# A deformable convolution behind a pair block: all sampling pairs of a unit ahead of the convolution of the same unit

## The chip, the cores and the metric

One core of one Trainium2 chip runs the whole program. The metric is device time in microseconds (us); a lower number is better. TensorE (PE) multiplies matrices, VectorE (DVE), ScalarE (ACT) and GpSimd (POOL) work elementwise, SyncE (SP) issues DMAs. Each engine runs its own list of instructions strictly in order, and waits at semaphores for the others.

## The reference

The input x has the shape (2, 128, 128, 128): 2 images, 128 channels, 128 x 128 pixels. Two layers are computed, each behind a group norm (32 groups of 4 channels) and each added to its input:

```
x = x + pair_block(group_norm(x))     # a, b, sigmoid gate: three 128x128 products,
                                      # a @ b per channel row, gate, product with Wo
x = x + deform_conv(group_norm(x))
def deform_conv(x):
    x = relu(x)
    offset = conv3x3(x, w_off) + b_off          # 18 channels: (y, x) for each of 9 taps
    py, px = pixel + tap + offset               # sampling places
    samp   = bilinear(x, py, px)                # zero outside the image
    return sum over channels and taps of samp * w_def
```

## The kernel before, in words

The first stage (about a fifth of the time) does the pair block in 64 groups and writes the sum to `x1_pad`. The second stage, the bands, does the deformable convolution and is what the change touches. An image is cut into 16 bands of 8 rows and each band into 2 sides of 64 columns: 64 units of 512 pixels for both images.

For one unit n, the steps are named by letters in a written list, `ORDER` (L404). All engines walk the same list; `bands` (L426) calls, for each step, only the function that the engine has for its letter. `ahead` (L428) says for which unit a letter works in turn n of the outer loop, relative to n. The letters:

- `h` near pixels: ScalarE norms and rectifies the 10 x 66 pixels around the unit (`cast_z`, L950), casts them to `z_hi` (L938), and VectorE makes the remainder `z_lo` (L1310).
- `O` offsets: TensorE convolves `z_hi` and `z_lo` with `woff` (L805), ScalarE takes the result out (L961).
- `P` VectorE splits the offsets into two float16 parts (L1273, L1276). `Q` TensorE turns them into distances between every sampling place and every pixel of its window (`locate`, L742 and L744), ScalarE takes their absolute value (`dist`, L970).
- `G` VectorE makes the bilinear hat functions (`hats`, L1284). `H` ScalarE's queue issues two DMAs that write them to memory (`store_hats`, L976). `R` VectorE takes the farthest distance (L1289), which the kernel looks at after the last band: no unit is far here, and a general path behind it doesn't run.
- SyncE spreads the hats over partitions (`spread_hats`, L545: three groups of three taps), GpSimd multiplies the y and x hats into `weights`, nine products a unit (`k`, `weigh`, L1541). Their first product waits until all pairs of the unit two before are sampled.
- `z` ScalarE makes `z`, the 22 overlapping windows of a unit (`make_z`, L927). `T` TensorE turns them, four windows a group and two in the last (L777); the groups are copied to `zT` by ScalarE (T0, T2, T4, L994) and VectorE (T1, T3, T5, L1319). A group's bank is free when the copy of the group two before is done.
- `s` sampling, eleven pairs of windows: four matmuls (L759) write a bank. ScalarE copies the high float16 part (`copy_samples`, L985), VectorE the low part (`copy_samples_lo`, L1300). Three banks take turns, so pair p waits for the low part of pair p - 3 (`lows_ready`, L755).
- `c` the nine taps of the convolution, three matmuls each (`conv`, L731). The first waits for all low parts of its unit. After the last, VectorE adds the input rows and writes `y` (`add_x1`, L1334).

Samples, weights and windows have two buffers each (`u = n % 2`), `zT`, the near pixels and the hats one. Rows of the input stand in a ring of 11 blocks of 4 rows (`raw`); SyncE loads a block when the unit that read its predecessor last has its `y` (L524), and stores a finished band (L533). Before the change the convolution works one unit behind the sampling (`"c": -1`), with taps written between the pairs. No planner is at work; the order is the one written out.

Of the kernel before, what the change touches and what calls it, by code (L numbers as in the profile page):

```python
# [7 lines left out]
P = 128  # L8
# [11 lines left out]
RPI, SIDES = HH // BR, WW // UW  # L20
BPI = RPI * SIDES
BANDS = IMGS * BPI
# [11 lines left out]
AHEAD = 3  # L34
# [64 lines left out]
def preact_conv_kernel(nc, x, Wa, ba, Wb, bb, Wg, bg, Wo, bo, w_off, b_off, w_def,  # L99
                       ident_d, group_mask_d, select_d, select_all_d, coords_d, out):  # L100
    with ExitStack() as ctx:
        def sb(name, shape, dt=F32):
            return ctx.enter_context(nc.sbuf_tensor(name, shape, dt))
# [63 lines left out]
        z = sb("z", [P, 2, WINDOWS, SRC_R, SRC_C])  # L167
# [15 lines left out]
        s6 = sb("s6", [P, BATCH, 6])  # L183
# [212 lines left out]
        def sampled_pair(b):  # L396
# [5 lines left out]


        ORDER = [(step[0], int(step[1:])) for step in (  # L404
            "h0 s0 s1 s2 k0 h1 c0 c1 T0 k1 s3 s4 z0 z1 O0 k2 s5 c2 c3 T1 k3 s6 P0 s7 c4 T2 k4 c5 s8 Q0 "
            "c6 k5 G0 T3 s9 k6 H0 c7 T4 k7 s10 c8 T5 k8 R0").split()]

        def hats_landed(n):

# [7 lines left out]
        def last_unit(block):  # L417

            b = min(block % BLOCKS // (BR // RB), RPI - 1)
            return block // BLOCKS * BPI + b * SIDES + SIDES - 1  # L420
# [4 lines left out]

        def bands(eng, stages):  # L426

            ahead = {"c": -1, "s": 0, "k": 1, "T": 1, "z": 2, "h": 3, "O": 3, "P": 3, "Q": 3,  # L428
                     "G": 3, "H": 3, "R": 3}
            for n in range(-AHEAD, BANDS + 1):  # L430
                for kind, j in ORDER:
                    m = n + ahead[kind]
                    if kind in stages and 0 <= m < BANDS:
                        stages[kind](m, m % 2, j)

        block = ctx.enter_context(nc.Block())
# [3 lines left out]
        def _(sp):  # L440
# [78 lines left out]
            def load_block(block):  # L519

                if block >= IMGS * BLOCKS:
                    return
                if block >= RING:
                    sp.wait_ge(y_ready, last_unit(block - RING) + 1)  # L524
                slot = block % RING
                sp.dma_start(raw[:, slot * RB:(slot + 1) * RB, :].rearrange("p r w -> p (r w)"),
                             x1_pad[block // BLOCKS, :, block % BLOCKS * RB:(block % BLOCKS + 1) * RB, :]
                             .rearrange("c r w -> c (r w)")).then_inc(raw_in[slot], 16)

            def store_y(n):  # L530
                b = n // SIDES
                sp.wait_ge(y_ready, n + 1)
                sp.dma_start(out_v[b // RPI, :, b % RPI * BR * WW:(b % RPI + 1) * BR * WW],  # L533
                             y[:, b % 2, :]).then_inc(y_out[b % 2], 16)

            def spread_hats(n):


                sp.wait_ge(*hats_landed(n))
                for g in range(TROWS):  # L540
                    wait(sp, weights_ready, TAPS * (n - 1) + TROWS * (g + 1))
                    rows = [hat_rows[0][n % AHEAD, g, g:g + NEAR_R].rearrange("(r o) c -> r o c", o=1),
                            hat_rows[1][n % AHEAD, g].rearrange("(o r) c -> o r c", o=1)]
                    for dst, src in zip((hy_flat, hx_flat), rows):
                        sp.dma_start(dst[g * SRC_C:(g + NEAR_R) * SRC_C,  # L545
                                         g * CHUNK:(g + 1) * CHUNK],
                                     src.broadcast_to([NEAR_R, SRC_C, CHUNK])
                                     ).then_inc(hat_in[g], 16)
# [4 lines left out]
            spread_hats(0)  # L553
            spread_hats(1)

            for n in range(BANDS + 2):
                if n >= 2 and n % SIDES == 1:
                    store_y(n - 2)
                for block in range(IMGS * BLOCKS):
                    if last_unit(block) == n - 2:  # L560
                        load_block(block + RING)
                if n + 2 < BANDS:
                    spread_hats(n + 2)
# [35 lines left out]
        def _(pe):  # L599
# [137 lines left out]
            def locate(n, u, _):  # L737

                pe.wait_ge(off_split, n + 1)
                wait(pe, dist_ready, n)  # L740
                for axis in range(2):
                    nc.tensor.matmul(pairs[0][:, axis, :], select[:, axis, :],  # L742
                                     offs_hi[:], start=True, stop=False)
                    mm = nc.tensor.matmul(pairs[0][:, axis, :], select[0:CONST_AT, axis, :],  # L744
                                          offs_lo[0:CONST_AT, :], start=False, stop=True)
                mm.then_inc(located, 1)
# [64 lines left out]
            def offsets(n, u, _):  # L811
                pe.wait_ge(z_hi_ready, n + 1)
                wait(pe, dist_ready, n)
                convolve_offset_parts(n).then_inc(off_done, 1)

            pe.wait_ge(select_set, SELECT_STEPS)
            pe.wait_ge(scaling, W_STEPS)
            bands(pe, {"c": conv, "Q": locate, "s": sample, "T": turn_windows, "O": offsets})


# [47 lines left out]
        def _(act):  # L868
# [89 lines left out]
            def evict_offsets(n, u, _):  # L958
                act.wait_ge(off_done, n + 1)
                wait(act, off_split, n)  # L960
                nc.scalar.activation(offs4[0:CONST_AT, :], bank[B_OFF][0:CONST_AT, :], ACT.Identity,  # L961
                                     bias=bias_off[0:CONST_AT, :],
                                     scale=unscale[0:CONST_AT, OFF:OFF + 1]
                                     ).then_inc(off_evicted, 1)
# [23 lines left out]
            def copy_windows(n, u, g):  # L988
                if g % 2:
# [8 lines left out]
            act.wait_ge(scaling, W_STEPS)  # L998
            act.wait_ge(final, FINAL_STEPS)
            bands(act, {"Q": distances, "H": store_hats, "s": copy_samples, "T": copy_windows,  # L1000
                        "z": make_z, "h": cast_z, "O": evict_offsets})


        @block.vector
        def _(dve):
# [316 lines left out]
            def add_x1(n, u, k):  # L1322
# [7 lines left out]
                for r0, r1, src in ((0, whole, at), (whole, BR, 0)):  # L1330
                    if r0 == r1:
# [10 lines left out]

            dve.wait_ge(scaling, W_STEPS)
            bands(dve, {"c": add_x1, "P": split_offsets, "G": make_hats, "R": reach_of,
                        "s": copy_samples_lo, "T": copy_windows, "h": split_z})

# [248 lines left out]
```

## Time and profile before

| | |
|---|---|
| median of 3 runs | 1642.09 us (1631.22 to 1646.17) |
| profiled execution | 1645.54 us, span 1643.7 us |
| TensorE, matmuls | busy 1543.9 us, 94% of the span |
| VectorE | 1111.5 us, 68% |
| ScalarE | 1052.1 us, 64% |
| GpSimd | 934.0 us, 57% |
| granted TensorE clock | 0.986 of full speed in the mean |
| band stage | first sampling matmul at 384.15 us, last tap at 1636.74 us |

Busy time is a union of an engine's instructions over the span. Matmuls are pipelined: one of 512 columns lasts 0.38 us from start to end, but the next starts 0.22 us after it. So on TensorE the differences of starts count, not durations. A row's idle time is time in which its engine did nothing ahead of it, and the arrow names what ended the wait.

### The profile page before, as it was taken

What the parts mean: (1) busy time and instruction counts of PE and PEld (TensorE: products, weight loads), DVE (VectorE), ACT (ScalarE), POOL (GpSimd) and SP (SyncE); (2) the same over time, 40 slices, a digit from 0 to 9 for tenths busy, and PEclk for the clock granted to TensorE, in tenths of its full rate; (3) what the DMA queues carried; (4) which work ended last, traced back from release to release, by engine and by line L of the source; (5) the groups of instructions that cost most, each with busy time, mean ns of one, the idle gap of its engine ahead of it and who ended that gap; (6) DMA issues with size and microseconds to landing.
All of it is one profiled execution on the core that took longest, in us unless ns stands there. A gap on an engine that the chain in (4) does not pass through costs nothing.

```text
span 1643.7 us, 28193 instructions
## 1 busy us (share of the span) xinstructions
PE 1543.9 (94%) x9875; PEld 1129.6 (69%) x9876; DVE 1111.5 (68%) x1910; ACT 1052.1 (64%) x1500; POOL 934.0 (57%) x734
## 2 busy tenths in 40 slices
PE   4999999937999999999999999999999999999997
PEld 3777787715776667776666676766777677767775
DVE  5988888745666666666666666666666666666653
ACT  2555555527676767767667666666777777666662
POOL 2555555716755555655665656566566566656562
PEclk9999999958999999999999999999999999999999
DMA  4343344246767777777776777777767777777672
GB/s 138 107 119 106 118 118 118 75 166 241 262 260 247 253 240 268 252 253 246 247 251 243 242 252 255 246 249 272 261 237 256 254 256 268 261 243 247 242 238 67
DMA packets 145701, 356.56 MB, mean 217 GB/s; under 512 B 10709, under 2 KB 77808, under 8 KB 145584
## 3 DMA queue, kind: packets, MB, share of 16 engines
q1 hardware_dynamic: 130864, 327.90, 59.1%
q10 hardware_dynamic: 14720, 27.14, 4.7%
q8 instruction: 69, 1.13, 0.3%
q14 instruction: 48, 0.39, 0.1%
HBM read 292.14 MB, written 62.85 MB: 216 GB/s over the span
## 4 chain that ended last, share of the span: by engine, by line
PE 61%; issue 12%; POOL 8%; DVE 8%; DMA 6%; ACT 2%; SPq 0%; ACTq 0%; POOLq 0%; DVEq 0%
PE bank L759 24%; PE pair L731 17%; PE pair L805 7%; DMA hx_all<-hat_x 6%; POOL samples_hi L1496 4%; PE bank L777 4%; DVE offs_lo L1276 3%; PE pair L777 3%; POOL weights L1541 2%; DVE offs_hi L1273 2%; PE pair L742 2%; PE pair L744 2%; ACT samples_hi L985 1%; POOL rstd L1470 1%; POOL samples_lo L1483 1%
## 5 line engine op out<-in xcount | busy, mean ns | idle before, releaser
L1541 POOL TENSOR_TENSOR weights<-hy_all,hx_all 126x512 f32<-126x512 f32 x576 | 756.6, 1343 | 522.0 <-DMA hx_all<-hat_x 381.6
L1300 DVE SCALAR_TENSOR_TENSOR samples_lo<-bank,samples_hi 128x432 f16<-128x432 f32 (+1 forms) x704 | 403.4, 591 | 364.7 <-ACT samples_hi L985 351.5
L759 PE MATMUL bank<-weights,zT 126*128 126x216 f32 (+1 forms) x2816 | 583.0, 344 | 2.7 <-POOL weights L1541 2.3
L759 PEld LDWEIGHTS bank<-weights,zT 126*128 126x128 f32 x2816 | 490.2, 190 | 44.0 <-issue 29.2
L985 ACT ACTIVATE samples_hi<-bank 128x432 f16<-128x432 f32 (+1 forms) x704 | 362.4, 519 | 226.3 <-PE bank L759 216.2
L731 PE MATMUL pair<-samples_hi,w_hi 128*128 128x512 f16 x576 | 218.9, 380 | 1.2 <-DVE y L1334 1.2
L731 PE MATMUL pair<-samples_lo,w_hi 128*128 128x512 f16 x576 | 217.7, 378 | 0.0
L731 PE MATMUL pair<-samples_hi,w_lo 128*128 128x512 f16 x576 | 217.6, 378 | 0.0
L994 ACT COPY zT<-pair 126x512 f32<-126x512 f32 x192 | 112.5, 586 | 112.2 <-PE pair L777 108.0
L927 ACT ACTIVATE z<-raw,norm_band 128x2772 f32<-128x2772 f32 (+3 forms) x80 | 180.0, 2270 | 0.0
L1483 POOL TENSOR_TENSOR samples_lo<-samples_hi,samples_lo 128x512 f16<-128x512 f32 x64 | 74.2, 1159 | 131.1 <-ACT samples_lo L888 131.0
L879 ACT ACTIVATE samples_hi<-pair,nbias,rstd 128x512 f32<-128x512 f32 x64 | 49.8, 778 | 135.3 <-PE pair L630 84.3
L777 PEld LDWEIGHTS pair<-ident,z 128*126 128x126 f32 x768 | 96.2, 141 | 36.9 <-issue 0.5
L1319 DVE COPY zT<-bank 126x512 f32<-126x512 f32 (+1 forms) x192 | 113.9, 593 | 5.0 <-PE bank L777 5.0
L777 PE MATMUL pair<-ident,z 128*126 128x128 f32 x768 | 116.1, 274 | 0.0
L950 ACT ACTIVATE abg_space<-raw,norm_band 128x660 f32<-128x660 f32 (+2 forms) x74 | 104.9, 1431 | 16.9 <-DMA raw<-x_pad 12.4
L777 PEld LDWEIGHTS bank<-ident,z 128*126 128x126 f32 x640 | 81.7, 140 | 40.3 <-DVE zT L1319 2.7
L805 PE MATMUL pair<-z_hi,woff 128*64 128x512 f16 x576 | 87.5, 412 | 17.8 <-ACT z_hi L938 17.8
L777 PE MATMUL bank<-ident,z 128*126 128x128 f32 x640 | 101.8, 274 | 2.3 <-DVE zT L1319 2.3
L731 PEld LDWEIGHTS pair<-samples_lo,w_hi 128*128 128x128 f16 x576 | 55.5, 96 | 69.0
L970 ACT ACTIVATE dist<-pair 128x1024 f32<-128x1024 f32 x64 | 65.6, 1025 | 57.0 <-PE pair L744 57.0
L1284 DVE TENSOR_SCALAR hats<-dist 128x1024 f32<-128x1024 f32 x64 | 52.4, 819 | 68.1 <-ACT dist L970 68.1
(138 smaller groups left out, 1944.8 us busy)
## 6 DMA issues: line engine op xcount, KB each, us to landing
hy_all<-hat_y SPq DMA_DIRECT2D x192, 648.0 KB
hx_all<-hat_x SPq DMA_DIRECT2D x192, 648.0 KB
raw<-x_pad SPq DMA_DIRECT2D x68, 272.0 KB, 11.2
x_pad<-hy_all SPq DMA_DIRECT2D x64, 272.0 KB, 3.3
weights<-in_x SPq DMA_DIRECT2D x64, 256.0 KB, 2.9
out<-y SPq DMA_DIRECT2D x32, 512.0 KB, 10.6
hat_y<-hats ACTq DMA_DIRECT2D x64, 252.0 KB
hat_x<-hats ACTq DMA_DIRECT2D x64, 162.0 KB
```

The source lines that it names most:

```text
L731: mm = nc.tensor.matmul(bank[B_CONV], w_part[:, k, :], part[:, u, k, :], start=(k == 0 and (w_part, part) == (w_hi, samples_hi)), stop=(k ...
L759: mm = nc.tensor.matmul(sampled_pair(b)[:, :, at:at + BR * cols], zT[0:WPIX, w, :], weights[0:WPIX, u, :, w * WC * BR:(w * WC + cols) * BR ...
L777: mm = nc.tensor.transpose(bank[B_ZT[g % 2]][0:WPIX, (w % 4) * P:(w % 4 + 1) * P], z[:, u, w].rearrange("p r c -> p (r c)"), ident[:])
L805: mm = nc.tensor.matmul(bank[B_OFF][at:at + width, :].rearrange("p (w r) -> p w r", r=BR), woff[:, k, 0:width], pixels[:, kx:kx + UW, ky:k ...
L927: done = nc.scalar.activation(z[:, u, :, rows, :], patches, ACT.Relu, bias=norm_band[:, 1].rearrange("p b n -> p (b n)")[:, n:n + 1], scal ...
L950: done = nc.scalar.activation(z_near[:, :, r0:r1], raw[:, src:src + r1 - r0, left:left + UW + 2].rearrange("p r w -> p w r"), ACT.Relu, bi ...
L985: nc.scalar.activation(samples_hi[:, u, :, c0:c1], sampled_pair(b)[:, :, 0:c1 - c0], ACT.Copy).then_inc(samples_ready, 1)
L994: nc.scalar.copy(zT[0:WPIX, 4 * g:4 * g + c, :].rearrange("p w c -> p (w c)"), bank[B_ZT[0]][0:WPIX, 0:c * P]).then_inc(zT_a, 1)
L1300: nc.vector.scalar_tensor_tensor(out=samples_lo[:, u, :, c0:c1], in0=sampled_pair(b)[:, :, 0:c1 - c0], scalar=1.0, in1=samples_hi[:, u, :, ...
L1319: nc.vector.tensor_copy(zT[0:WPIX, 4 * g:4 * g + c, :].rearrange("p w c -> p (w c)"), bank[B_ZT[1]][0:WPIX, 0:c * P]).then_inc(zT_v, 1)
L1483: nc.gpsimd.tensor_tensor(xT_lo[:], xT[:], xT_hi[:], ALU.subtract).then_inc(xT_lo_ready, 1)
L1541: nc.gpsimd.tensor_tensor(weights[0:WPIX, u, k, :], hy_all[0:WPIX, k, :], hx_all[0:WPIX, k, :], ALU.mult).then_inc(weights_ready, 1)
```

## The change

The list `ORDER` is written anew: the eleven pairs of a unit come first, then the offsets, then the nine taps of the same unit (`"c": 0`), among which turns, offsets, locating and distances lie. The near pixels are made four units ahead in place of three, at the end of the turn in place of its start and middle. The outer loop begins one turn earlier and ends one earlier. SyncE's stores and row loads follow the convolution, which is one turn earlier by the loop's count.

```diff
         ORDER = [(step[0], int(step[1:])) for step in (
-            "h0 s0 s1 s2 k0 h1 c0 c1 T0 k1 s3 s4 z0 z1 O0 k2 s5 c2 c3 T1 k3 s6 P0 s7 c4 T2 k4 c5 s8 Q0 "
-            "c6 k5 G0 T3 s9 k6 H0 c7 T4 k7 s10 c8 T5 k8 R0").split()]
+            "s0 s1 k0 s2 s3 k1 s4 s5 k2 s6 s7 k3 s8 s9 s10 O0 k4 z0 z1 c0 c1 T0 P0 c2 T1 k5 c3 c4 T2 Q0 c5 T3 "
+            "G0 k6 c6 h0 T4 H0 c7 k7 h1 T5 c8 k8 R0").split()]
...
-            ahead = {"c": -1, "s": 0, "k": 1, "T": 1, "z": 2, "h": 3, "O": 3, "P": 3, "Q": 3,
+            ahead = {"c": 0, "s": 0, "k": 1, "T": 1, "z": 2, "h": 4, "O": 3, "P": 3, "Q": 3,
                      "G": 3, "H": 3, "R": 3}
-            for n in range(-AHEAD, BANDS + 1):
+            for n in range(-AHEAD - 1, BANDS):
                 for kind, j in ORDER:
...
-            for n in range(BANDS + 2):
-                if n >= 2 and n % SIDES == 1:
-                    store_y(n - 2)
+            for n in range(BANDS + 1):
+                if n >= 2 and n % SIDES == 0:
+                    store_y(n - 1)
                 for block in range(IMGS * BLOCKS):
-                    if last_unit(block) == n - 2:
+                    if last_unit(block) == n - 1:
                         load_block(block + RING)
```

## Rows read from the trace of the kernel before

**Rows 1.** Busy time by stretch, band stage: PE, PEld, DVE, ACT, POOL, clock, DMA share, GB/s

```profile
1160.00:1360.00 200.00, 199.24 (x1188) 142.52 (x1184) 131.72 (x208) 141.47 (x200) 119.29 (x92) 1.00 0.74 251
```

**Rows 2.** Timeline of TensorE, one turn: start us, duration us, engine, line, operation

```profile
1197.06 1.32 PE L805 MATMUL pair<-z_hi,woff 128*64 128x512 f16 x9
...
1199.12 1.00 PE L759 MATMUL bank<-weights,zT 126*128 126x216 f32 x4
...
1205.61 0.38 PE L742 MATMUL pair<-offs_hi,select 117*128 117x512 f16 x1
...
1206.49 0.38 PE L731 MATMUL pair<-samples_hi,w_hi 128*128 128x512 f16 x1
...
1209.39 0.70 PE L759 MATMUL bank<-weights,zT 126*128 126x216 f32 x4
1209.93 0.38 PE L731 MATMUL pair<-samples_hi,w_hi 128*128 128x512 f16 x1
...
1210.58 0.38 PE L777 MATMUL bank<-ident,z 128*126 128x128 f32 x2
1210.80 2.36 PE L759 MATMUL bank<-weights,zT 126*128 126x216 f32 x12
1212.99 0.38 PE L731 MATMUL pair<-samples_hi,w_hi 128*128 128x512 f16 x1
...
1216.28 1.32 PE L805 MATMUL pair<-z_hi,woff 128*64 128x512 f16 x9
```

**Rows 3.** Timeline of ScalarE, the same turn; idle time before in brackets

```profile
1197.59 2.74 ACT L927 ACTIVATE z<-raw,norm_band 128x2772 f32<-128x2772 f32 x1
1200.23 0.78 ACT L961 ACTIVATE offs<-pair,bias_off,unscale 114x512 f32<-114x512 f32 x1
...
1206.69 1.02 ACT L970 ACTIVATE dist<-pair 128x1024 f32<-128x1024 f32 x1 [0.34 <-PE pair L744]
1208.51 0.53 ACT L985 ACTIVATE samples_hi<-bank 128x432 f16<-128x432 f32 x1 [0.79 <-PE bank L759]
...
1209.59 0.59 ACT L994 COPY zT<-pair 126x512 f32<-126x512 f32 x1 [0.56 <-PE pair L777]
...
1210.44 1.59 ACT L950 ACTIVATE abg_space<-raw,norm_band 128x660 f32<-128x660 f32 x1
...
1213.62 0.75 ACT L938 ACTIVATE z_hi<-abg_space 128x660 f16<-128x660 f32 x1
```

**Rows 4.** Timeline of ScalarE and its DMA queue, in the ramp of the bands

```profile
383.26 0.31 ACTq L976 DMA_DIRECT2D hat_y<-hats  x1
383.61 0.45 ACTq L976 DMA_DIRECT2D hat_x<-hats  x1
384.10 0.59 ACT L994 COPY zT<-pair 126x512 f32<-126x512 f32 x1 [1.60 <-DVE hats L1284]
```

**Rows 5.** Timeline of VectorE, an undivided y; T5's copy and R lie between

```profile
1191.73 0.74 DVE L1334 SCALAR_TENSOR_TENSOR y<-pair,unscale,raw 128x512 f32<-128x512 f32 x1
...
1193.55 1.64 DVE L1300 SCALAR_TENSOR_TENSOR samples_lo<-bank,samples_hi 128x432 f16<-128x432 f32 x3
```

**Rows 6.** By line, 420 to 1600 us: ns min/median/max; and a timeline row of GpSimd

```profile
L1284 DVE TENSOR_SCALAR hats<-dist x59: 693/695/1677, 438.0 to 1578.5; 128x1024 f32<-128x1024 f32 x59
L1276 DVE TENSOR_TENSOR offs_lo<-offs,offs_hi x59: 691/1634/1645, 434.1 to 1574.9; 114x512 f16<-114x512 f32 x59
L1310 DVE TENSOR_TENSOR z_lo<-abg_space,z_hi x59: 835/1098/1946, 425.0 to 1566.0; 128x660 f16<-128x660 f32 x59
...
1152.10 11.74 POOL L1541 TENSOR_TENSOR weights<-hy_all,hx_all 126x512 f32<-126x512 f32 x9 [3.57 <-PE bank L759]
```

**Rows 7.** Timeline of TensorE: a locate in the ramp, the first pairs, the last tap

```profile
380.39 0.39 PE L742 MATMUL pair<-offs_hi,select 117*128 117x512 f16 x1 [2.06 <-DVE offs_lo L1276]
...
384.15 2.36 PE L759 MATMUL bank<-weights,zT 126*128 126x216 f32 x12
...
1636.74 0.38 PE L731 MATMUL pair<-samples_lo,w_hi 128*128 128x512 f16 x1
```

## The prediction

> **What bounds the kernel now.** First the stretches of busy time: in 200 us of the band stage TensorE is busy 199.24 us at a granted clock of 1.00, VectorE 131.72, ScalarE 141.47, GpSimd 119.29 [rows 1]. So TensorE's own list of work sets the length of a turn there, and the other engines have 60 to 80 us of slack in 200. Whether that slack lies in the right place is what the change alters. Second, TensorE's timeline of one turn: it issues without a hole for 19.22 us [rows 2]. From the differences of starts: offsets (O) 2.06 us; locate (Q) 0.88; one tap of the convolution, three matmuls, 0.65; a group of two window turns 0.22, so 0.43 for four; three sampling pairs 2.19, so 0.73 a pair; the short last pair 0.54. A turn is then 2.06 + 9 x 0.65 + 5.5 x 0.43 + 0.88 + 10 x 0.73 + 0.54 = 19.0 us, and no order of it can be shorter. Third, ScalarE and VectorE in the same kind of turn [rows 3 to 5]: what each pair needs behind TensorE, and what else these two do between pairs.
>
> **What the change does to a turn.** No instruction is added or removed. All eleven pairs s0 to s10 come first, then O, nine taps among T0 to T5, Q, and the rest. Pair p writes one of three banks and waits until VectorE has taken the low part of pair p-3 (`lows_ready`). Before, taps lie between pairs and give ScalarE and VectorE time; after, three pairs may run and the fourth has to wait for the chain of the first.
>
> *The sampling run by itself.* From the start of a pair: 0.73 + 0.17 until its result is out (the row of twelve matmuls ends 0.17 after the next start [rows 2]), 0.53 high part on ScalarE [rows 3], 0.61 low part on VectorE (the last of the three in 1.64 us, which follow each other by 0.52 [rows 5]), with 0.03 to 0.05 at each hand-over: 2.15 us, against 2.19 for three pairs. So the run costs nothing as long as both engines are free for it. The join s10 to c0 costs nothing either: high and low of the short pair take about 1.2 us, and O covers them with 2.06 (in the last turns, which have no O, that cover is gone and c0 comes 1.25 us late).
>
> *The rest of the turn, which now stands in one block.* I walk it from the start of O, t = 0. **TensorE** if nothing is late: O to 2.06, c0 c1 to 3.36, T0 3.79, c2 T1 4.87, c3 c4 6.17. **ScalarE**: the offsets leave at 2.06 + 0.17 + 0.03 = 2.26, for 0.77 [rows 3]; z0/z1 2.74 us, started 0.1 before its predecessor ends as there, so 2.93 to 5.67; only then the copy of T0, 5.57 to 6.16. T2 waits for it: 6.21 to 6.64 on TensorE, 0.04 late. Q to 7.52. (VectorE's P0 is done in time: from 3.06 a cast and offs_lo, each at most the 1.64 us of [rows 6], give 6.4, and Q starts at 6.64.) Distances 1.02 from 7.72 to 8.74; h0 1.59, 8.64 to 10.23; T4's copy 0.59, 10.13 to 10.72 (turned at 9.88); H0, the two DMA issues of the hats, which stand in ScalarE's queue: from the first issue to the next instruction 0.84 [rows 4], so 10.75 to 11.59; h1's z_hi 0.75 [rows 3], to 12.34. **VectorE** is behind that in order: h1's z_lo, then T5's copy, y (needs c8), the reach R0, and only then the low part of s0 of the next unit. z_lo from 12.37; I take 1.25 us, between the median 1.10 and the longest 1.95 [rows 6], since GpSimd will run there more often (below): 13.62. y, T5's copy and R0 together take 1.82 us up to the next low part from the start of y to that of the low parts [rows 5]; another order, the same sum: 13.54 to 15.36. Low part of s0: 15.97. s3 can start at 16.0.
>
> TensorE without this wait: c5 T3 c6 T4 to 9.68, c7 T5 c8 to 11.20, s0 s1 s2 to 13.39. So **s3 stands for 2.6 us in every turn**, with the whole of TensorE's queue behind it. Low parts of s1 and s2 follow at 0.52 us, faster than the pairs, and the rest of the run is undisturbed: s3 to s10 take 7 x 0.73 + 0.54 = 5.65. The new turn is 16.0 + 5.65 = **21.65 us** against 19.0 of pure work. Pieces of z, near pixels and y split at the end of the ring of rows add something; 0.1 a turn is my estimate, 21.75.
>
> *Moves past queues.* GpSimd may start the products of the unit after next when all eleven pairs of a unit are sampled (`sampled`); that point comes nearly at the start of the block, where it was late in the turn. Nine products take 11.74 us [rows 6], and are now due a whole turn later: no cost by itself. SyncE's store and row loads are renumbered by one with the convolution; they wait for the same y at the end of a turn, next to the hats that SyncE needs anyway: nothing. The earlier near pixels ask for ring rows whose predecessors were freed three turns or more before: nothing.
>
> *Locks between VectorE and GpSimd.* The rows show hats at 0.69 us in the median and 1.68 at most, offs_lo 0.69 to 1.64, z_lo 0.84 to 1.95 [rows 6]. An undisturbed product of GpSimd is 1.30 us (11.74 / 9), and every excess is at most about that. As the nine products now begin near t = 0.2, they cover the block up to t = 12 or later, where offs, hats and z_lo lie. Hats run from 9.35 (after T3's copy): at 0.7 us they end before H0 could be issued, at 1.68 they end at 11.03 and push H0 by 0.3. Without any such delay z_lo takes 0.84 and the turn is 21.2; with the full one at both places it is 21.65 + 0.3 + 0.7 = 22.65.
> The Trainium skill ("SBUF — State Buffer", the section on the shared port pair) says that VectorE and GpSimd hold one pair of ports as an exclusive lock for a whole instruction and the loser blocks fully. The spread of those rows agrees. It speaks against this change, as it makes the long end (22.65) the more likely one; the sum above stays at the value between.
>
> **The sum.** The first pair starts at 384.15 and the last tap's last matmul at 1636.74 [rows 7]; 1643.7 - 1636.96 = 6.74 us follow. Nothing ahead of the first pair changes materially. After: 384.15 + 7.84 (first eleven pairs) + 60 turns with near pixels and offsets x 21.75 = 1305 + one turn without near pixels 19.2 + two without offsets and locate 17.35 each (1.25 + 5.85 + 2.4 + 7.84) + the last nine taps 1.25 + 5.85 + 6.74 = 1764.7. The profiled execution took 1645.5 for a span of 1643.7, so 1.8 more: about **1767 us**; its own time is 0.2% above the median of the three runs, which I ignore. Ends: turn 20.5, if no lock bites (21.2) and the 0.84 of the DMA issues holds nothing up: 1692 us. Turn 22.8 with full locks and split pieces: 1830.
>
> **Rivals.**
> (a) *The block fits, and TensorE stays full.* Mechanism: if ScalarE and VectorE get through the block 2.6 us sooner, s3 never waits, and the small holes before Q vanish as well. The turn is 19.03: 1767 - 60 x 2.72 = 1604 us. It decides at one point: the low part of s0 must be done by 13.35, where I have 15.97. For it: 60 us of slack in 200. Against: the chain O, z, T0, T2, Q, distances, near pixels, H0, z_hi, z_lo, tail is serial, each link measured. 0.06.
> (b) *Half of it fits.* The wait is 0.3 to 0.8 us a turn, and the gain of fewer holes before Q eats it: 1625 to 1655. 0.05.
> (c) *The clock falls.* TensorE now pauses once a turn. In the ramp it had idled 2.06 us before a locate which ran at 0.39 us a matmul, the full clock [rows 7]; I expect 2.6 to behave alike. If the sampling behind the wait ran at half clock, it took 5.65 us more a turn: 1767 + 339 = 2106. 0.03.
> [...]
> (d) *The wait comes, of another size.* Short (1692 to 1735, no locks, issues cheap) 0.17; as summed (1735 to 1800) 0.52; long (1800 to 1830) 0.17.
>
> **Numbers.** About 1% is what a measurement of this kernel can tell from no change. (d) and (c) are slower: 0.89. (b) is mostly within 1%: 0.05. (a) is faster: 0.06. The range 1692 to 1830 holds (d), 0.86, and leaves out the rest.
>
> **What would show it.** Right: in every turn the fourth pair (L759) idles 2 to 3.5 us, released by VectorE's low part; just ahead of it VectorE runs z_lo, zT, y, farthest, low part without a hole; TensorE is at about 88% in the stage; no hole before Q; granted clock still 1.00; GpSimd released by TensorE in nearly all turns. Wrong: low part of s0 directly behind its high part, or holes elsewhere (T2 or T4 waiting for zT, sampling waiting for weights). The prediction fails if ScalarE does not hold up z_hi until the hats are issued, or if z_lo and the tail of VectorE overlap more than their rows say.

## The result and the profile after

The changed kernel takes 1846.01 us in the median of 6 runs (1834.02 to 1852.09); the kernel before, now also with 6 runs, 1640.76 us. The ratio is 1.1229, with a 95% interval of 1.1186 to 1.1272. Medians are over all runs and ratios over the fast ones alone, since a program now and then runs about a per cent slower, whatever the kernel. The forecast was slower, 1767 us, range 1692 to 1830: the direction and the wait of the fourth pair came true, the clock did not, and the size lies outside the range. The profiled execution took 1852.1 us, 85.6 more than the sum of 1766.5 that the prediction made for it.

First the page of the changed kernel (span, TensorE's busy time, and the sampling matmuls with the idle time ahead of them), and the stretch of 200 us that answers to [rows 1]:

```profile
span 1850.3 us, 28193 instructions
...
PE 1630.8 (88%) x9875; PEld 1202.5 (65%) x9876; DVE 1133.6 (61%) x1910; ACT 1068.4 (58%) x1500; POOL 953.3 (52%) x734
...
L759 PE MATMUL bank<-weights,zT 126*128 126x216 f32 (+1 forms) x2816 | 611.5, 378 | 144.8 <-DVE samples_lo L1300 136.7
```

```profile
1200.00:1400.00 200.00, 181.92 (x1031) 130.32 (x1030) 117.03 (x177) 125.11 (x173) 113.93 (x84) 0.97 0.64 221
```

TensorE idles 136.7 us for VectorE's low parts, where it had 0.4 before. Its share is 88% of the span and 90% over the 60 turns with offsets, near the 88% expected. But that is 137 us, and the span is 207 us longer; and the granted clock, 1.00 before, is 0.97 in this stretch and 0.95 over the 60 turns. The timeline of TensorE shows both losses. Two turns, each from its fourth pair (the row with the idle time in brackets) over the offsets (L805) to the three pairs ahead of the next wait:

```profile
1199.48 6.18 PE L759 MATMUL bank<-weights,zT 126*128 126x216 f32 x32 [1.39 <-DVE samples_lo L1300]
1205.60 1.32 PE L805 MATMUL pair<-z_hi,woff 128*64 128x512 f16 x9
...
1216.77 2.35 PE L759 MATMUL bank<-weights,zT 126*128 126x216 f32 x12
1221.12 7.73 PE L759 MATMUL bank<-weights,zT 126*128 126x216 f32 x32 [2.00 <-DVE samples_lo L1300]
1228.79 1.32 PE L805 MATMUL pair<-z_hi,woff 128*64 128x512 f16 x9
```

The same eight pairs take 6.12 us up to the next offsets behind a pause of 1.39 us, and 7.67 behind one of 2.00. In three short stretches around the second (columns as in [rows 1]):

```profile
1219.12:1221.12 2.00, 0.01 (x1) 0.00 (x0) 1.94 (x4) 0.53 (x1) 2.00 (x3) 1.00 0.28 113
...
1221.12:1224.20 3.08, 3.08 (x12) 2.94 (x13) 1.91 (x4) 1.06 (x2) 1.19 (x1) 0.69 0.95 311
1224.20:1228.79 4.59, 4.59 (x23) 4.16 (x22) 2.72 (x5) 2.62 (x5) 0.00 (x0) 0.84 0.74 259
```

The clock is granted in full during the pause; behind it, the mean is 0.69 and then 0.84 of full speed, a mix of the two levels of 2.4 and 1.2 GHz. I took the 58 turns from 443.99 to 1781.46 us apart in this way; a turn here runs from one start of the offsets to the next. Mean turn 23.06 us: fourth pair at 15.88 us after the start of the offsets, pause 2.28 (1.39 to 3.33), and from the fourth pair to the next offsets 7.18. The last number is 6.11 in 21 turns and 7.5 to 9.0 in 37; the latter are called slow below.

Why the fourth pair waits: ScalarE and VectorE in the turn from 1205.60 (t = 0).

```profile
1211.08 0.57 ACT L994 COPY zT<-pair 126x512 f32<-126x512 f32 x1
1212.41 0.59 ACT L994 COPY zT<-pair 126x512 f32<-126x512 f32 x1 [0.76 <-PE pair L777]
1213.29 1.02 ACT L970 ACTIVATE dist<-pair 128x1024 f32<-128x1024 f32 x1 [0.29 <-PE pair L744]
1214.21 1.62 ACT L950 ACTIVATE abg_space<-raw,norm_band 128x660 f32<-128x660 f32 x1
1215.70 0.31 ACTq L976 DMA_DIRECT2D hat_y<-hats  x1
1215.72 0.59 ACT L994 COPY zT<-pair 126x512 f32<-126x512 f32 x1
1216.05 0.34 ACTq L976 DMA_DIRECT2D hat_x<-hats  x1
1216.49 0.75 ACT L938 ACTIVATE z_hi<-abg_space 128x660 f16<-128x660 f32 x1 [0.18 <-issue]
```

```profile
1217.28 1.45 DVE L1310 TENSOR_TENSOR z_lo<-abg_space,z_hi 128x660 f16<-128x660 f32 x1 [1.61 <-ACT z_hi L938]
1218.65 0.41 DVE L1319 COPY zT<-bank 126x256 f32<-126x256 f32 x1
1218.99 0.73 DVE L1334 SCALAR_TENSOR_TENSOR y<-pair,unscale,raw 128x512 f32<-128x512 f32 x1
1219.75 0.68 DVE L1289 TENSOR_REDUCE farthest<-dist 18x1 f32<-18x512 f32 x1
1220.46 1.64 DVE L1300 SCALAR_TENSOR_TENSOR samples_lo<-bank,samples_hi 128x432 f16<-128x432 f32 x3
```

This is the chain that the prediction walked, link by link. ScalarE has only 0.18 us of holes between distances and z_hi, and VectorE none from z_lo to the first low part, which ends at 1221.1 and releases the fourth pair at 1221.12. (A lock is what the prediction calls it when VectorE's and GpSimd's instructions lengthen each other.) One turn later it shows: hats take 1.52 us, the DMA issues start 0.58 after the start of T4's copy (0.02 before it in the turn above), z_hi waits 0.81 "for hats", and the pause becomes 2.83. Of these 0.83 us more, 0.2 are the near pixels (L950), which run in two pieces here. In 10 of 59 turns z_hi waits for the hats, 10.5 us in all.

```profile
1238.18 1.52 DVE L1284 TENSOR_SCALAR hats<-dist 128x1024 f32<-128x1024 f32 x1
1239.15 0.57 ACT L994 COPY zT<-pair 126x512 f32<-126x512 f32 x1
1239.73 0.31 ACTq L976 DMA_DIRECT2D hat_y<-hats  x1
...
1240.52 0.75 ACT L938 ACTIVATE z_hi<-abg_space 128x660 f16<-128x660 f32 x1 [0.81 <-DVE hats L1284]
```

### The profile page after: what moved, and what is told of

The parts are those of the page before. It is cut to its first block, busy times and chain, and to the rows that moved or that the text cites. A ratio compares the mean times of both kernels' runs of the same rounds, so it can differ in the third digit from the quotient of the medians.

```text
span 1850.3 us, 28193 instructions
## 1 busy us (share of the span) xinstructions
PE 1630.8 (88%) x9875; PEld 1202.5 (65%) x9876; DVE 1133.6 (61%) x1910; ACT 1068.4 (58%) x1500; POOL 953.3 (52%) x734
## 4 chain that ended last, share of the span: by engine, by line
PE 51%; issue 18%; DVE 10%; ACT 10%; POOL 6%; ACTq 2%; DMA 1%; SPq 0%; DVEq 0%; POOLq 0%
PE bank L759 25%; PE pair L731 10%; PE pair L805 7%; ACT abg_space L950 4%; POOL samples_hi L1496 4%; PE pair L777 3%; ACT z_hi L938 2%; DVE y L1334 2%; DVE farthest L1289 2%; DVE samples_lo L1300 2%; ACT z L927 2%; PE bank L777 2%; PE pair L744 2%; PE pair L742 1%; ACTq L976 1%
## 5 line engine op out<-in xcount | busy, mean ns | idle before, releaser
L1541 POOL TENSOR_TENSOR weights<-hy_all,hx_all 126x512 f32<-126x512 f32 x576 | 775.9, 1376 | 702.2 <-DMA hx_all<-hat_x 655.2
L759 PE MATMUL bank<-weights,zT 126*128 126x216 f32 (+1 forms) x2816 | 611.5, 378 | 144.8 <-DVE samples_lo L1300 136.7
L759 PEld LDWEIGHTS bank<-weights,zT 126*128 126x128 f32 x2816 | 559.1, 210 | 209.1 <-DVE samples_lo L1300 157.1
L1310 DVE TENSOR_TENSOR z_lo<-abg_space,z_hi 128x660 f16<-128x660 f32 x64 | 85.6, 1338 | 107.0 <-ACT z_hi L938 107.0
L879 ACT ACTIVATE samples_hi<-pair,nbias,rstd 128x512 f32<-128x512 f32 x64 | 49.8, 778 | 136.6 <-PE pair L630 85.6
L777 PEld LDWEIGHTS pair<-ident,z 128*126 128x126 f32 x768 | 91.4, 140 | 48.8 <-ACT zT L994 23.5
L1273 DVE CAST offs_hi<-offs 114x512 f16<-114x512 f32 x64 | 45.5, 711 | 125.2 <-ACT offs L961 125.2
L961 ACT ACTIVATE offs<-pair,bias_off,unscale 114x512 f32<-114x512 f32 x64 | 49.8, 778 | 115.2 <-PE pair L805 115.2
L950 ACT ACTIVATE abg_space<-raw,norm_band 128x660 f32<-128x660 f32 (+2 forms) x74 | 105.1, 1435 | 12.1 <-DMA raw<-x_pad 12.1
```

Source lines behind the costliest of these rows:

```text
L759: mm = nc.tensor.matmul(sampled_pair(b)[:, :, at:at + BR * cols], zT[0:WPIX, w, :], weights[0:WPIX, u, :, w * WC * BR:(w * WC + cols) * BR ...
L777: mm = nc.tensor.transpose(bank[B_ZT[g % 2]][0:WPIX, (w % 4) * P:(w % 4 + 1) * P], z[:, u, w].rearrange("p r c -> p (r c)"), ident[:])
L950: done = nc.scalar.activation(z_near[:, :, r0:r1], raw[:, src:src + r1 - r0, left:left + UW + 2].rearrange("p r w -> p w r"), ACT.Relu, bi ...
L1310: nc.vector.tensor_tensor(z_lo[:], z_near[:], z_hi[:], ALU.subtract).then_inc(z_lo_ready, 1)
L1541: nc.gpsimd.tensor_tensor(weights[0:WPIX, u, k, :], hy_all[0:WPIX, k, :], hx_all[0:WPIX, k, :], ALU.mult).then_inc(weights_ready, 1)
```

## The experiments

The theory behind all of them: in each turn VectorE's serial tail holds the fourth pair (A); a pause of about 2 us and more often lets the clock fall for the pairs behind it (B); locks with GpSimd lengthen and scatter the tail (C). Rivals: something else holds the pair, or the slow pairs come from DMA traffic, or the lead of the near pixels or the same-unit taps cost by themselves. Each ratio is against the kernel before, run at the same time (medians 1641 to 1650 us), with its 95% interval. Mean turns are taken from the start of the first unit's offsets pass among the pairs to that of the last, over 60 turns; before 19.65, changed 23.04. For near_ahead_behind none is given, since its profiled execution (1681.7 us) was one of its longest.

| run | median us | ratio | turn us |
|---|---|---|---|
| changed kernel | 1846.0 | 1.123 (1.119 to 1.127) | 23.04 |
| fill | 1793.5 | 1.090 (1.085 to 1.095) | 21.96 |
| fill_half | 1795.3 | 1.088 (1.083 to 1.093) | 22.08 |
| reach_later | 1736.9 | 1.054 (1.049 to 1.058) | 21.31 |
| issue_later | 1760.1 | 1.066 (1.054 to 1.078) | 21.40 |
| fewer_products | 1774.7 | 1.078 (1.073 to 1.082) | 21.63 |
| tail_short | 1661.3 | 1.008 (1.004 to 1.011) | 19.85 |
| unit_behind | 1848.0 | 1.122 (1.116 to 1.129) | 23.06 |
| near_ahead | 1768.5 | 1.073 (1.069 to 1.078) | 21.73 |
| near_ahead_behind | 1664.2 | 1.007 (1.002 to 1.012) | - |
| locate_later | 1647.3 | 0.997 (0.993 to 1.001) | 19.64 |
| offsets_sooner | 1638.5 | 0.989 (0.980 to 0.998) | 19.46 |

**Is it the clock? (fill, fill_half)**

```diff
             def sample(n, u, p):
                 b = p % 3
+                if p == 3:
+                    wait(pe, dist_ready, n + 3 if n + 3 < BANDS else BANDS)
+                    for _ in range(FILL):        # 10, or 5
+                        nc.tensor.matmul(pairs[0][:, 0, :], w_hi[:, 0, :], w_hi[:, 1:5, :],
+                                         start=True, stop=True)
```

> The changed kernel with ten extra matmuls of 512 columns (10 x 0.22 = 2.2 us) between the third and the fourth pair of every unit; they write a bank that nobody reads then, so the output is as before. Theory (the pause of 2.28 us lets the clock fall, and the pairs behind it run slowly): the fourth pair starts as late as before, near t = 15.9, but the stretch from it to the offsets takes 6.1 us in all turns instead of 7.18 in the mean; the turn falls from 23.06 to about 22.0 and the time from 1846 to about 1786. Rival 1 (the slow pairs come from DMA traffic or reads of the weights at that moment): stretch and time stay, 1846 or a little more. Rival 2 (TensorE's own work is what counts): plus 60 x 2.2, 1978.

> As the run with ten extra matmuls, but with five (1.1 us) between the third and the fourth pair, so that about 1.2 us of pause are left (0.3 to 2.2). If the length of the pause alone decides on the clock, nearly no turn is slow behind it, since all pauses below 1.7 us in the changed kernel were followed by a full clock: 22.05 us a turn, about 1790. If the clock answers to how much TensorE works in the turn as a whole, about half of the loss of 1.07 us a turn stays: about 1815.

With ten, TensorE does 2.2 us more a turn, and the kernel becomes 3% faster than the changed one. In the profile of fill, the pairs from the fourth on come straight behind the extra matmuls (L754; the sampling is L765 there) and take 6.0 us:

```profile
800.32 2.36 PE L765 MATMUL bank<-weights,zT 126*128 126x216 f32 x12
802.51 2.32 PE L754 MATMUL pair<-w_hi 128*128 128x512 f16 x10
804.67 6.08 PE L765 MATMUL bank<-weights,zT 126*128 126x216 f32 x32
810.68 1.32 PE L811 MATMUL pair<-z_hi,woff 128*64 128x512 f16 x9
```

None of its 60 turns is slow behind the wait, with the fourth pair as late as ever (15.88), and the granted clock of the whole execution is 0.986, against 0.947. So B holds: the slow pairs are the clock's, and they cost 1.1 us a turn. Traffic by itself is out: weights, hats and rows move as before. fill_half leaves 1.21 us of pause in the mean, and only 3 of 58 turns are slow; the first reading of its expectation, by what is left of the pause, is the one that fits. It is not the whole rule, as the count shows. Over the turns of six kernels (changed, unit_behind, reach_later, fill_half, fewer_products, issue_later), a slow stretch came behind none of 197 pauses below 1.75 us, 7 of 24 from there to 2.0, 61 of 100 from 2.0 to 2.5, and 37 of 39 above.

**Is it VectorE's tail? (reach_later, issue_later, tail_short)**

```diff
-  ... s9 s10 O0 ... T4 H0 c7 k7 h1 T5 c8 k8 R0        # changed kernel
+  ... s9 s10 R0 O0 ... T4 H0 c7 k7 h1 T5 c8 k8        # reach_later ("R": 2)
+  ... s9 s10 O0 ... T4 h1 c7 k7 H0 T5 c8 k8 R0        # issue_later
+  ... s9 s10 y0 R0 O0 ... T4 h1 H0 c7 k7 T5 c8 k8     # tail_short ("R": 2, "y": -1)
```

(tail_short gives the addition of y its own letter, one turn later, with SyncE's stores and loads as in the kernel before.)

> The changed kernel with the reach reduction R0 (0.68 us on VectorE) moved from VectorE's tail ahead of the low part of s0 to behind the low part of s10. Theory (VectorE's serial tail sets the start of the fourth pair, and longer pauses cost clock too): the fourth pair starts 0.68 us sooner, 60 turns x 0.68 = 41 us, and with pauses of 1.6 us in the mean fewer turns are slow behind it, another 30 to 45 us: about 1765. With the tail alone and no effect on the clock: 1805. Rival (ScalarE or the weights set it): 1846.

> The changed kernel with H0 (ScalarE's wait for the hats and its two DMA issues) behind z_hi and one tap further, in place of ahead of z_hi. Theory (the issues, and the hats that GpSimd's lock delays, hold up z_hi in ScalarE's queue and so VectorE's tail): the fourth pair starts 0.4 to 0.6 us sooner, with less scatter, and fewer turns are slow behind it: about 1790, 1770 to 1805. Rival (z_hi waits for something else): 1846.

> The changed kernel with its tail shortened: y and the reach R0 moved behind the low part of s10, and z_hi ahead of the hats' DMA issues (row loads and stores of SyncE one turn later). Theory: VectorE's tail is only z_lo and T5's copy; the fourth pair starts at t = 13.8 in place of 15.9, the pause is 0.4 us, the clock stays full and the turn is 19.9: about 1657 us, near the kernel before but not below it, since a run of pairs by itself takes 6.1 us behind the fourth, not 5.65. If something else but VectorE's tail holds the fourth pair: above 1700.

reach_later moves one instruction of 0.68 us from ahead of the low part to behind s10, and gains 109 us in the medians; 71 to 86 were expected. The fourth pair starts at 15.05 in place of 15.88 (0.83, of which 0.68 is expected; the rest I did not trace), and only 6 of 58 turns are slow behind it, which takes the stretch to the next offsets from 7.18 to 6.27. So 0.83 us of tail cost 1.74 us a turn. issue_later: fourth pair at 15.10, 6.30 behind it, 86 us gained, more than the 41 to 76 expected. Over the 58 turns z_hi starts at 10.69 in the mean in place of 11.33, which is 0.64 sooner, and z_lo is 0.15 shorter: together the 0.78 by which the fourth pair moved. The turns in which z_hi waits for the hats, as in the second one above, are part of the 0.64. tail_short closes nearly all of the loss with order alone; no work is taken out. Its fourth pair starts at 13.74, and no turn is slow behind it. Its VectorE goes from z_lo and T5's copy straight to the low parts, and its TensorE runs all eleven pairs in one piece:

```profile
706.81 0.85 DVE L1310 TENSOR_TENSOR z_lo<-abg_space,z_hi 128x660 f16<-128x660 f32 x1 [1.31 <-ACT z_hi L938]
707.57 0.42 DVE L1319 COPY zT<-bank 126x256 f32<-126x256 f32 x1
708.09 2.07 DVE L1300 SCALAR_TENSOR_TENSOR samples_lo<-bank,samples_hi 128x432 f16<-128x432 f32 x3
```

```profile
706.60 8.34 PE L759 MATMUL bank<-weights,zT 126*128 126x216 f32 x44
```

That is A, shown by removal: expected 1657, measured 1661.

**Are the locks real? (fewer_products)**

```diff
+                c = BW if n < 2 or k % TROWS == 0 else 8
                 nc.gpsimd.tensor_tensor(weights[0:WPIX, u, k, 0:c], hy_all[0:WPIX, k, 0:c], ...
```

> The changed kernel with less work on GpSimd: from the third unit on, six of nine products of weights are made for 8 of 512 columns only (the rest of these weights stay those of the first two units). Waits and DMAs are as before; GpSimd is busy about 4 us a turn in place of 12. Theory (locks between VectorE and GpSimd lengthen VectorE's tail and make it vary): z_lo 0.85 us in place of 1.45, hats 0.69 in all turns, the fourth pair 0.6 to 0.8 us sooner and with little scatter, fewer slow turns behind it: about 1750. Rival (no locks, z_lo is slow for another reason): 1846.

It leaves out most of the weights (six of nine products are made for 8 of 512 columns), so its output is not the layer's; it serves for its times alone. The median of z_lo falls to what it is alone, first the changed kernel, then this one (ns, min/median/max):

```profile
L1310 DVE TENSOR_TENSOR z_lo<-abg_space,z_hi x51: 845/1446/1903, 432.5 to 1581.3; 128x660 f16<-128x660 f32 x51
```

```profile
L1310 DVE TENSOR_TENSOR z_lo<-abg_space,z_hi x55: 845/847/1876, 426.8 to 1594.3; 128x660 f16<-128x660 f32 x55
```

The fourth pair starts at 15.25, 0.63 sooner, 10 of 58 turns are slow behind it, and the turn is 1.4 us shorter. That z_lo grows shorter when GpSimd works less is the lock, and C holds; the total is 25 us above the 1750 expected. The one product in three that is left still meets z_lo or hats now and then (the maximum stays).

**Lag and lead by themselves (unit_behind, near_ahead, near_ahead_behind)**

```diff
+  "c": -1, outer loop and SyncE as before, the changed kernel's ORDER      # unit_behind
+  kernel before, "h": 4, range(-AHEAD - 1, BANDS + 1)                      # near_ahead
+  near_ahead, h1 moved from behind k0 to behind O0                        # near_ahead_behind
```

> The changed kernel's order, but with the taps of the unit before (convolution one unit behind, as in the kernel before), outer loop and SyncE to match. Theory (the grouping of eleven pairs costs, not that the taps are of the same unit): 1846 within 10 us, pause and stretch as in the changed kernel. Rival (the taps wait for the low part of the last pair): the pause between s10 and c0 would go, and the time fall by more than 1%.

> The kernel before with one thing of the change alone: near pixels four units ahead, at their old places in the order, the outer loop one turn longer at its start. Theory (the lead costs nothing): 1641 within 8 us. Rival (the lead costs, through ring rows or the ramp): over 1657.

> The kernel before with near pixels four units ahead, and h1 (z_hi, z_lo) moved from behind k0 to behind O0. The run with the lead alone was 7% slower, and its ScalarE waits 4.8 us a turn at z_hi for the offsets of the unit before, which stand behind it in the same turn and read the one buffer. Theory (a wait of order, not the lead): with h1 behind O0 that wait is gone, 1641 within 15 us. Rival (the lead itself costs): above 1700.

unit_behind: no difference; that the taps are of the same unit costs nothing, the grouping does. near_ahead went against the expectation: 7% slower. In its profile ScalarE stands at z_hi until the offsets of the unit before are through, which now come later in the same turn and read the one z_hi buffer:

```profile
632.33 1.32 PE L805 MATMUL pair<-z_hi,woff 128*64 128x512 f16 x9
633.58 0.88 PE L805 MATMUL pair<-z_lo,woff 128*32 128x512 f16 x9
```

```profile
634.55 0.75 ACT L938 ACTIVATE z_hi<-abg_space 128x660 f16<-128x660 f32 x1 [4.78 <-PE pair L805]
```

near_ahead_behind keeps the lead, moves h1 behind O0, and takes the wait away with 1.007. So the lead is nearly free, but it binds the place of h1: by the same wait the change could not have kept h1 ahead of the offsets (argued, not run), and its place at the end of the turn is what loads the tail. The 0.7% that is left I did not test; in the profiled execution TensorE waits 68.9 us in all for the low offsets ahead of Q0 (L742), in the kernel before 26.4.

**Is there anything to win in the kernel before? (locate_later, offsets_sooner)**

```diff
-  k3 s6 P0 s7 c4 T2 k4 c5 s8 Q0 c6 k5 G0
+  k3 s6 P0 s7 c4 T2 k4 c5 s8 c6 Q0 k5 G0      # locate_later
+  k3 P0 s6 s7 c4 T2 k4 c5 s8 Q0 c6 k5 G0      # offsets_sooner
```

> The kernel before with one edit: TensorE's Q0 behind the next tap c6 in place of ahead of it. In the kernel before, Q0 waits for the low offsets in about half of the turns, 0.2 to 0.95 us. Theory: a tap of 0.65 us covers most of it, and nothing that hangs on Q0 is needed soon: 19.3 us a turn in place of 19.67, 1 to 1.5% faster, 1617 to 1630. Rival (distances and hats come later and delay the spread of hats, which then holds up GpSimd and the sampling): no change or slower.

> The kernel before with VectorE's P0 (split of the offsets) ahead of the low part of s6 in place of behind it. Theory: the low offsets are done about 1 us sooner, the hole before Q0 (0.2 to 1.2 us in half of the turns) closes as in the run with Q0 later, but distances and hats come sooner, not later: at best 19.25 us a turn and 1620. Rival (the spread of hats by DMA and GpSimd's products need about 19.6 us a turn by themselves, whatever TensorE's holes are): same as before, with waits for weights in place of the holes.

The waits of TensorE over 400 to 1560 us (total, times, longest), of the kernel before, of locate_later, and of offsets_sooner:

```profile
PE pair L742 <- DVE offs_lo L1276: 18.1, 27, 1.2
...
PE bank L759 <- POOL weights L1541: 0.4, 2, 0.2
```

```profile
PE bank L759 <- POOL weights L1541: 11.2, 6, 5.1
...
PE pair L742 <- DVE offs_lo L1276: 3.2, 8, 1.1
```

```profile
PE bank L759 <- POOL weights L1541: 7.8, 6, 3.2
...
PE pair L742 <- DVE offs_lo L1276: 2.1, 1, 2.1
```

Both nearly close the hole before Q0. With Q0 later, TensorE waits for weights instead and nothing is gained, where 1 to 1.5% were expected. With P0 sooner the ratio is 1.1% better than before (interval 0.2 to 2.0%), from few runs and with an interval that ends near zero: a hint rather than a settled gain, and less than the 1620 us and 19.25 us a turn that were the best case. Part of it again turns into waits for weights. That the weights are late because the hats are is the rival that both expectations named; it fits, and no run isolates it.

## Why the prediction was right and wrong

**The wait for the fourth pair: right.** Position 16.0 forecast, 15.88 measured; pause 2.6 against 2.28 (a row's idle time starts only with the end of the last matmul, 0.17 later than the forecast counted). The serial block, the DMA issues that hold z_hi, the 1.8 us of T5's copy, y and reach, the lock at hats and z_lo, and the covered join from s10 to c0 all stand in the trace. tail_short removed the wait and with it the loss.

**The clock: wrong, and the largest miss.** By itself it takes the sum from 1767 to 1831, just past the upper end of the range; the smaller misses below take it further. The failed step is rival (c): "In the ramp it had idled 2.06 us before a locate which ran at 0.39 us a matmul, the full clock; I expect 2.6 to behave alike", with a chance of 0.03. One pause of 2.06 us with a full clock behind it proved nothing for 2.6, and hardly for 2.06: from 2.0 to 2.5 us, 39 of 100 pauses end that way. And the row was read without what stands around it. In the ramp of the kernel before, TensorE has a wait of 2.06 us ahead of a locate three times. Behind the two others the matmuls take 0.61 us, and the clock stood at 0.50 of full speed until that third wait began (the last two rows are stretches, with the columns of [rows 1]):

```profile
351.72 0.61 PE L742 MATMUL pair<-offs_hi,select 117*128 117x512 f16 x1 [2.06 <-DVE offs_lo L1276]
364.72 0.61 PE L742 MATMUL pair<-offs_hi,select 117*128 117x512 f16 x1 [2.06 <-DVE offs_lo L1276]
...
376.37:378.33 1.96, 1.96 (x9) 1.56 (x8) 0.81 (x2) 0.78 (x1) 1.96 (x3) 0.50 0.00 1
378.33:380.39 2.06, 0.01 (x1) 0.00 (x0) 1.97 (x2) 0.59 (x1) 1.00 (x1) 0.95 0.77 307
```

So the row shows a clock that had just risen, after work at the lower level, and not one that outlived a pause after work at the full one. The clock had to be a term of the sum. The Trainium skill ("TensorE: Matmul & The Clock Gate", Part 1) says that an idle stretch returns the array to half rate; the runs agree, and show it behind pauses from 1.84 us on, shorter than those the page warns of. The price of (c) was wrong too: 5.65 us in all turns, 339 in all. Measured is 1.4 to 2.9 us in 37 of 58 turns, 7.18 - 6.11 = 1.07 in the mean, 64 us over 60 turns; removing it gave 1.08 us a turn (fill).

**The run of pairs: mis-sized.** Seven pairs and the short one were to take 5.65 us; at full clock they take 6.11, 0.46 x 60 = 28 us. The first pairs showed three in 2.19, since they need not wait. In the run, the chain of a bank is 2.32, not 2.15:

```profile
1199.48 2.12 PEld L759 LDWEIGHTS bank<-weights,zT 126*128 126x128 f32 x12 [1.73 <-DVE samples_lo L1300]
1201.80 3.72 PEld L759 LDWEIGHTS bank<-weights,zT 126*128 126x128 f32 x20 [0.20 <-issue]
```

The weight load of a pair that has to wait starts with the wait's end and no longer hides behind the pair before; a load lasts 0.19 us in the mean on the page of the kernel before. This I read from the rows and did not test. It explains about half of the 0.46 us; the rest lies in the last two pairs, untraced.

**The sum, closed.** The 60 turns take 1382.6 us in place of 1305, 77.6 more; the first pair is 4.2 later, at 388.31; the first eleven pairs take 10.5 in place of 7.84, 2.7; and the end, behind the last offsets, 1.1: 85.6. Most of the 2.7 is the clock again: behind an idle time of 8.16 us the first three pairs take 4.47 us at a granted clock of 0.50. Why the first pair is late I did not trace. Of the 58 turns (mean 23.06 against 21.75), the 1.31 is 1.07 clock + 0.46 run - 0.12 earlier fourth pair - 0.1 allowance for split pieces.

**GpSimd: wrong, without effect on the sum's sign.** I had it released by TensorE, with its products from t = 0.2. It waits for the spread of hats 655 us in all, and its last six products of the turn shown run from 1213.82 to 1222.3, right over hats, z_lo and y. The lock was met for another reason than the one given.

**Neutral edits.** Taps of the same unit: right, zero (unit_behind). Near pixels four ahead: zero was right for ring rows, but the reason why they must then stand behind O0 was missed; it explains why the tail has z_hi and z_lo in it at all.

## What to carry to other kernels

When work is grouped by kind on the busiest engine, the helpers' work becomes a serial chain in one gap; walk that chain, then ask what the busiest engine's clock does across the pause. Price a recurring idle of about 2 us on TensorE at its length plus the slow matmuls behind it; a row that shows the clock unharmed is no rule, and says nothing before one has looked at the clock ahead of it. Of a helper's tail, move out first what nobody waits for: one reduction of 0.68 us gave 109 us here.

## What the runs showed of the hardware

Ten matmuls of no use in a pause (2.2 us a turn) made the changed kernel 3% faster, and five did as well. Whether a pause of 2.0 to 2.5 us costs is not settled by its length: 61 of 100 did. Of the 105 slow stretches, 99 lost 1.4 to 1.55 us (7.47 to 7.66 for the eight pairs) and 6 about 2.9 (8.9 to 9.0); none lay between.
